# A top-2 mixture-of-experts block behind adapters: GpSimd's row scatters of the first six pairs alternate with its other work

## The chip, the cores and the metric

The kernel runs as one program on one core of a Trainium2 chip. The metric is the device time of one launch in microseconds (us). The kernel before was timed three times; its median is 654.41 us.

## The reference, cut to what matters

There are 16 sequences of 256 tokens with 256 features, 4096 tokens in all. Each sequence picks one of 8 adapters, passes it and a layer norm, and then each token passes a shared feed-forward network and the two best of 8 experts. Only the expressions that the kernel's stages carry out are kept:

```
z = relu(hidden @ Wd + bd)                      # adapter of the sequence, 256 -> 128
y = hidden + z @ Wu + bu
h = (y - mu) * rsqrt(var + eps) * g + b          # layer norm of the adapter's profile
p = softmax(h @ gate_w + gate_b)                 # 8 experts
v, idx = top_k(p, 2);  v = v / (sum(v) + 1e-9)
moe = sum_k v_k * (gelu(h @ ew1[idx_k] + eb1[idx_k]) @ ew2[idx_k] + eb2[idx_k])
out = x + h + gelu(h @ sh_w1 + sh_b1) @ sh_w2 + sh_b2 + moe   # 256 -> 1024 -> 256
```

## The kernel before, in words

All large products are made of fp16 halves: a value is split into a high and a low half, and three products of halves (high-high, high-low, low-high) are summed in fp32.

**Two stages.** The first stage goes through the sequences in eight pairs of 512 tokens (pair p holds sequences 2p and 2p+1). It makes adapter, norm, router and shared network, and writes each token's row (both halves of its normed features, its two expert weights, its number) twice into a table in memory, `xs_rows`, at the place that its two experts give it. The second stage runs the experts over tiles of that table and adds the results into the output.

**Steps.** The first stage is written as a row of steps s = -7 to 31, and each engine runs its own instructions of a step in the written order. Pair p starts at step base(p) = 7p/2 - 7, rounded down, so that about three pairs are in flight. From step 4 on, a step holds for TensorE 12 matmuls of the shared network's first product (L1158), 24 of its second product (L1170), and small work of the pairs. For ScalarE a step holds two GELUs (L554) and the high half of the hidden values (L562). For VectorE it ends with their low half (L966).

**One pair's chain.** The numbers are steps after base(p):

- 0 and 1: GpSimd adds the bias of the adapter to the input (`xb`, L403). TensorE makes down and up products (L1100, L1111).
- 2 and 3: VectorE takes statistics (L734, L737); GpSimd takes the root (`root`, L408).
- 4: VectorE finishes the scales (L752 to L758), ScalarE normalizes (L501).
- 5: VectorE multiplies by the gain (L764), GpSimd adds the norm's bias (`rows`, L413, one instruction for each sequence), ScalarE rounds the high half (L509), which needs both `rows` of the pair.
- 6: VectorE makes the low half (L768), SyncE issues four transposing DMAs (L287), GpSimd adds the residual (`residual`, L417, two instructions) and writes token numbers (L422).
- 8 (7 for the last two pairs): TensorE makes the router's logits (L1124, L1126); they need the transposes and the positions of the pair before (L808). One step later VectorE picks the two experts (L775 to L797) and ScalarE takes the exponentials (L513).
- 11 (10 for the last two): VectorE works out positions and weights (L803 to L832). Then the rows can be scattered.

**The scatters.** `scatter(p, i)` issues two indirect DMAs from GpSimd, one for each of the two experts, for token block i (0 to 3) of pair p (L430). Pair p has eight of them, 64 in all. In the kernel before, the pairs 0 to 5 issue two at the end of each of the steps 11 to 14 after base(p), behind all else that GpSimd has in the step:

```
for i in range(4):
    if s == base(p) + (11 + i if p < NP - 2 else 10 + i // 2):
        scatter(p, i)
```

Where two pairs meet in a step, four stand in a row. The pairs 6 and 7 issue four at the end of each of two steps. Later stages wait for scatters by counting semaphores of the pair's buffer (`d_row`); the buffers of a pair are used again three pairs later.

Of the kernel before, what the change touches and what calls it, by code (L numbers as in the profile page):

```python
# [17 lines left out]
NP = B // 2  # L18
# [20 lines left out]
def at(s, o):  # L39

    return [p for p in range(NP) if s - base(p) == o]
# [34 lines left out]
def adaln_moe(nc, x, xt, ids, wpack, vecs, gnb, gate_w, gate_b, w1, w2, b1, b2, out):  # L76
    ctx = ExitStack()
    with ctx:
# [305 lines left out]
        def gpsimd_program(pool):  # L384
# [21 lines left out]
            def root(p):  # L406
                pool.wait_ge(v_var, p + 1)
                pool.tensor_tensor(rs[:, p % 2, 1, :], rs[:, p % 2, 0, :], half[:, :], ALU.pow).then_inc(q_root, 1)  # L408

            def rows(b):  # L410
                pool.wait_ge(v_t, b + 1)
                y = yb_of(b).rearrange("p (j d) -> p j d", j=2)
                pool.tensor_tensor(y, y, bc(gbs[:, b % 4, 1:2, :], [P, 2, D]), ALU.add).then_inc(q_xn, 1)  # L413

            def residual(b):
                pool.wait_ge(q_xn, b + 1)
                pool.tensor_tensor(acc_of(b), acc_of(b), yb_of(b).rearrange("p (j d) -> p j d", j=2), ALU.add).then_inc(q_acc, 1)  # L417
# [3 lines left out]
                    pool.wait_ge(d_row[p % 3], 16 * 8 * (p // 3))  # L421
                pool.iota(xr[:, p % 3, :, 2 * D + 6:RH].bitcast(I32), pattern=[[P, 4], [0, 1]], base=512 * p, channel_multiplier=1).then_inc(q_tok, 1)  # L422

            def scatter(p, i):
                pool.wait_ge(v_pos, p + 1)
                pool.wait_ge(v_meta, p + 1)
                pool.wait_ge(v_xl, p + 1)
                pool.wait_ge(q_tok, p + 1)
                for q in range(2):
                    pool.indirect_dma_start(xs_d, bass.IndirectOffsetOnAxis(pos[:, p % 3, i, q:q + 1], 0), xr[:, p % 3, i, :].bitcast(I32), None).then_inc(d_row[p % 3], 16)  # L430

            for s in range(FIRST, NS):
                for p in at(s, 3):
                    root(p)
                for p in at(s, 5):
                    rows(2 * p)
                    rows(2 * p + 1)
                for p in at(s, 0):
                    xb(2 * p)
                for p in at(s, 1):  # L440
                    xb(2 * p + 1)
                for p in at(s, 6):
                    residual(2 * p)
                    residual(2 * p + 1)
                    tokens(p)
                for p in range(NP):
                    for i in range(4):
                        if s == base(p) + (11 + i if p < NP - 2 else 10 + i // 2):
                            scatter(p, i)

            def weigh_bias(n):
                pool.wait_ge(v_sel, n + 1)
# [849 lines left out]
```

## Time and profile before

| what | value |
|---|---|
| median of three runs | 654.41 us (653.47 to 654.74) |
| profiled execution | 652.95 us |
| its span, first to last instruction | 650.9 us |
| TensorE busy | 599.8 us, 92% |
| VectorE busy | 503.1 us, 77% |
| GpSimd busy | 413.1 us, 63% |
| ScalarE busy | 389.3 us, 60% |
| granted clock of TensorE, mean of the span | 0.976 |

The profiled execution took 652.95 us, of which 2.05 us lie outside of the span. The first stage lasts until about 243.5 us of the span, the experts take the rest. "Busy" counts an instruction from its recorded start to its recorded end, so time in which a started instruction waits for something inside of the core counts as busy. PE is TensorE, DVE is VectorE, ACT is ScalarE, POOL is GpSimd, and SPq is the DMA queue that SyncE fills.

### The profile page before, as it was taken

How to read it: one execution, taken by the hardware profiler on the slowest of the kernel's cores; microseconds unless marked ns; L12 is line 12 of the kernel's file. 1: busy time of each engine (PE TensorE's matmuls, PEld its weight loads, DVE VectorE, ACT ScalarE, POOL GpSimd, SP SyncE). 2: the span in 40 equal slices, each digit the busy share in tenths (PEclk: the TensorE clock that was granted, in tenths of full speed). 3: DMA queues.
4: the chain of work that ended last, by engine and by line, in shares of the span. 5: the costliest groups of instructions: out<-in, count | busy, mean ns of one | idle time of the engine just before them, and what ended most of it. 6: DMA issues, size and time to landing. Idle time of an engine off the chain costs nothing.

```text
span 650.9 us, 16857 instructions
## 1 busy us (share of the span) xinstructions
PE 599.8 (92%) x5073; PEld 484.5 (74%) x5073; DVE 503.1 (77%) x1198; ACT 389.3 (60%) x662; POOL 413.1 (63%) x320
## 2 busy tenths in 40 slices
PE   4356999999989899999999999999999999999994
PEld 2223666766646668888888888888888888889883
DVE  3859889979975793898989898988896665656883
ACT  1638666667767774667675858576754444434641
POOL 2435687788887601285959585858688575756743
PEclk9768999999989999999999999999999999999998
DMA  7964467666144756367657585666686342424410
GB/s 265 304 145 133 128 190 151 215 195 154 57 126 121 247 160 191 84 125 134 147 105 155 126 142 130 137 133 129 90 71 73 52 73 44 67 41 59 69 26 3
DMA packets 116740, 81.31 MB, mean 125 GB/s; under 512 B 71090, under 2 KB 106162, under 8 KB 116658
## 3 DMA queue, kind: packets, MB, share of 16 engines
q1 hardware_dynamic: 101346, 61.16, 38.4%
q0 software_dynamic: 13296, 16.92, 15.3%
q10 hardware_dynamic: 2016, 2.16, 1.1%
q8 instruction: 48, 0.79, 0.5%
q14 instruction: 34, 0.28, 0.2%
HBM read 43.21 MB, written 24.42 MB: 104 GB/s over the span
## 4 chain that ended last, share of the span: by engine, by line
PE 71%; DVE 9%; issue 7%; POOL 4%; ACT 3%; DMA 3%; SPq 2%; POOLq 0%; ACTq 0%; DVEq 0%
PE H L1219 29%; PE Y L1235 29%; PE Y L1170 6%; PE H L1158 6%; SPq L287 2%; POOL xs_rows L430 2%; DVE wreg L768 1%; DMA xT<-wreg 1%; POOL wreg L413 1%; DVE wreg L737 1%; DMA wreg<-in_wpack 1%; DVE wreg L734 1%; DVE wreg L828 1%; ACT hf L554 1%; ACT wreg L501 1%
## 5 line engine op out<-in xcount | busy, mean ns | idle before, releaser
L608 ACT ACTIVATE hf<-H,prme 128x256 f32<-128x256 f32 (+1 forms) x312 | 151.0, 541 | 112.1 <-issue 97.4
L1219 PE MATMUL H<-xT,wreg 128*128 128x256 f16 (+1 forms) x1872 | 200.4, 263 | 0.2
L1235 PE MATMUL Y<-wreg,hh 128*128 x1136 | 188.6, 273 | 3.6 <-issue 2.4
L1219 PEld LDWEIGHTS H<-xT,wreg 128*128 x1872 | 171.9, 98 | 21.1 <-issue 0.7
L1235 PE MATMUL Y<-wreg,hl 128*128 x568 | 154.8, 273 | 0.0
L1235 PEld LDWEIGHTS Y<-wreg,hh 128*128 128x128 f16 x1136 | 111.0, 98 | 20.6 <-issue 6.1
L1031 DVE SCALAR_TENSOR_TENSOR hl<-hf,prme,hh 128x512 f16<-128x512 f32 (+1 forms) x156 | 115.1, 738 | 5.6
L1029 DVE TENSOR_SCALAR hh<-hf,prme 128x512 f16<-128x512 f32 (+1 forms) x156 | 84.6, 542 | 40.4 <-ACT hf L608 38.3
L457 POOL TENSOR_SCALAR b2w<-b2t,wsel 128x256 f32<-128x256 f32 x71 | 99.1, 1606 | 23.6 <-DMA b2t<-in_b 18.1
L1158 PE MATMUL H<-xT,wreg 128*128 128x512 f16 x384 | 93.8, 396 | 11.8 <-DMA xT<-wreg 11.7
L468 POOL DMA_INDIRECT out_y<-hh,xgm x36 | 64.7, 1799 | 58.0 <-DVE hh L1057 38.9
L468 POOL DMA_INDIRECT out_y<-hl,xgm x35 | 63.6, 1819 | 53.7 <-DVE hl L1057 40.2
L430 POOL DMA_INDIRECT xs_rows<-wreg x64 | 70.1, 1096 | 25.9 <-issue 25.9
L1170 PE MATMUL Y<-wreg,hh 128*128 128x256 f16 x512 | 85.4, 273 | 0.4 <-DVE hl L966 0.4
L1158 PEld LDWEIGHTS H<-xT,wreg 128*128 128x128 f16 x384 | 37.9, 101 | 57.2 <-DMA xT<-wreg 12.8
L1170 PE MATMUL Y<-wreg,hl 128*128 128x256 f16 x256 | 69.8, 273 | 0.0
L554 ACT ACTIVATE hf<-H,prm 128x512 f32<-128x512 f32 x64 | 47.6, 772 | 35.7 <-PE H L1158 28.1
L461 POOL TENSOR_TENSOR b2w<-b2w,xT 128x512 f32<-128x512 f32 (+1 forms) x39 | 53.3, 1367 | 21.9 <-ACT xT L618 19.3
L966 DVE SCALAR_TENSOR_TENSOR hl<-hf,prm,hh 128x1024 f16<-128x1024 f32 x32 | 45.5, 1423 | 25.7 <-ACT hh L562 21.8
L1235 PEld LDWEIGHTS Y<-wreg,hl 128*128 128x128 f16 x568 | 55.6, 98 | 6.0
L1170 PEld LDWEIGHTS Y<-wreg,hh 128*128 128x128 f16 x512 | 50.0, 98 | 12.8 <-issue 1.0
L545 ACT ACTIVATE wreg<-stage,sm 128x2048 f16<-128x2048 f32 x18 | 36.0, 1999 | 38.7 <-DVE prmr L722 23.2
(189 smaller groups left out, 672.9 us busy)
## 6 DMA issues: line engine op xcount, KB each, us to landing
stage<-in_w SPq DMA_DIRECT2D x16, 1024.0 KB
b2t<-in_b SPq DMA_DIRECT2D x39, 128.0 KB
wreg<-in_wpack SPq DMA_DIRECT2D x16, 256.5 KB
wreg<-in_xt SPq DMA_DIRECT2D x16, 256.0 KB
wreg<-in_x SPq DMA_DIRECT2D x16, 256.0 KB, 5.6
wreg<-in_vecs SPq DMA_DIRECT2D x16, 256.0 KB, 4.0
out_y<-wreg SPq DMA_DIRECT2D x16, 256.0 KB, 2.2
xs_rows<-wreg SPq DMA_DIRECT2D x9, 260.0 KB
```

Source lines behind the costliest of these rows:

```text
L430: pool.indirect_dma_start(xs_d, bass.IndirectOffsetOnAxis(pos[:, p % 3, i, q:q + 1], 0), xr[:, p % 3, i, :].bitcast(I32), None).then_inc(d ...
L457: pool.tensor_scalar(b2w[:, n % 2, j, :], b2t[:, n % 3, :], wsel[:, n % 4, 0, j:j + 1], None, ALU.mult).then_inc(q_b2, 1)
L461: pool.tensor_tensor(w, w, b2f[:, 0:blocks(n), :], ALU.add).then_inc(q_b2, 1)
L468: pool.indirect_dma_start(out_rows, bass.IndirectOffsetOnAxis(xgm[:, n % 6, j, 3:4].bitcast(I32), 0), yo_of(n)[:, j, :], None, bounds_chec ...
L554: act.activation(hf[:, g % 4, :], H[g % 3][:, :], ACT.Gelu_apprx_tanh, bias=pr[:, c:c + 1], scale=pr[:, 8:9]).then_inc(a_g, 1)
L608: act.activation(hf[:, c, half * w:(half + 1) * w], H[c][:, half * w:(half + 1) * w], ACT.Gelu_apprx_tanh, bias=pr[:, ch:ch + 1], scale=pr ...
L1029: dve.tensor_scalar(hh[:, n % 2, dst], hf[:, c, 0:w], pr[:, 9:10], None, ALU.mult).then_inc(v_own, 1)
L1031: dve.scalar_tensor_tensor(hl[:, n % 2, dst], hf[:, c, 0:w], pr[:, 9:10], hh[:, n % 2, dst], ALU.mult, ALU.subtract).then_inc(ve_lo, 1)
L1158: m = pe.matmul(H[g % 3][:, :], wsh[:, 0, h, k * 1024 + c * P:k * 1024 + c * P + P], xp[:, a + k, :], start=n == 0, stop=n == 5)
L1170: m = pe.matmul(Y[b % 2][:, j % 2 * D:(j % 2 + 1) * D], hx[:, t % 2, c * 512 + j * P:c * 512 + (j + 1) * P], wsh[:, 1, h, c * D:(c + 1) * ...
L1219: m = pe.matmul(H[c][:, half * w:(half + 1) * w], we[:, bass.ds(e + h * 2048 + k * 1024 + col, P)], xp[:, a + k, 0:w], start=i == 0, stop= ...
L1235: m = pe.matmul(Y[n % 2][:, j * D:(j + 1) * D], hx[:, n % 2, c * w + j * P:c * w + (j + 1) * P], we[:, bass.ds(e + 4096 + h * 2048 + c * D ...
```

## The change

The eight scatters of each of the pairs 0 to 5 are no longer issued two by two at the ends of four steps. They are spread singly over the steps 11 to 15 after base(p), in front of, between and behind the two `rows`, the two `residual`, the `xb` and the `root` that other pairs have in these steps. Even and odd pairs have slots of their own. At most two stand in a row, but for one place with three (steps 20 and 21) and the end of pair 5 (steps 24 and 25), where GpSimd has nothing else left but the scatters of pair 6. An even pair issues its first scatter in step 11 and its last in step 14, an odd pair in the steps 12 and 15. The semaphore waits stand at a pair's first scatter alone. The pairs 6 and 7 issue theirs as before. Nothing is added or removed: 64 scatters and all other instructions are the same.

```diff
-            def scatter(p, i):
-                pool.wait_ge(v_pos, p + 1)
-                pool.wait_ge(v_meta, p + 1)
-                pool.wait_ge(v_xl, p + 1)
-                pool.wait_ge(q_tok, p + 1)
-                for q in range(2):
-                    pool.indirect_dma_start(xs_d, bass.IndirectOffsetOnAxis(pos[:, p % 3, i, q:q + 1], 0), xr[:, p % 3, i, :].bitcast(I32), None).then_inc(d_row[p % 3], 16)
+            def scatter(p, i, q):
+                if (i, q) == (0, 0):
+                    pool.wait_ge(v_pos, p + 1)
+                    pool.wait_ge(v_meta, p + 1)
+                    pool.wait_ge(v_xl, p + 1)
+                    pool.wait_ge(q_tok, p + 1)
+                pool.indirect_dma_start(xs_d, bass.IndirectOffsetOnAxis(pos[:, p % 3, i, q:q + 1], 0), xr[:, p % 3, i, :].bitcast(I32), None).then_inc(d_row[p % 3], 16)
+
+            def even(s, o, i, q):
+                for p in at(s, o):
+                    if p % 2 == 0 and p < NP - 2:
+                        scatter(p, i, q)
 ...
             for s in range(FIRST, NS):
+                even(s, 14, 3, 0)
+                odd(s, 15, 3, 1)
                 for p in at(s, 3):
                     root(p)
+                odd(s, 14, 2, 1)
+                even(s, 13, 1, 1)
                 for p in at(s, 5):
                     rows(2 * p)
+                odd(s, 12, 0, 0)
+                even(s, 12, 0, 1)
+                for p in at(s, 5):
                     rows(2 * p + 1)
+                odd(s, 12, 0, 1)
+                even(s, 12, 1, 0)
                 for p in at(s, 0):
                     xb(2 * p)
                 for p in at(s, 1):
                     xb(2 * p + 1)
+                even(s, 14, 3, 1)
+                odd(s, 12, 1, 0)
+                odd(s, 14, 3, 0)
+                even(s, 11, 0, 0)
                 for p in at(s, 6):
                     residual(2 * p)
+                odd(s, 13, 1, 1)
+                even(s, 13, 2, 0)
+                for p in at(s, 6):
                     residual(2 * p + 1)
                     tokens(p)
-                for p in range(NP):
+                odd(s, 13, 2, 0)
+                even(s, 13, 2, 1)
+                for p in range(NP - 2, NP):
                     for i in range(4):
-                        if s == base(p) + (11 + i if p < NP - 2 else 10 + i // 2):
-                            scatter(p, i)
+                        if s == base(p) + 10 + i // 2:
+                            scatter(p, i, 0)
+                            scatter(p, i, 1)
```

`odd` is written like `even`, for the odd pairs. Only GpSimd's order changes; the other engines keep theirs.

On GpSimd, the steps 7 to 9 before read as follows (L430 is a scatter, L403 `xb`, L413 `rows`, L417 `residual`; the four scatters are the last two of pair 0 and the first two of pair 1):

```order
L403 TENSOR_TENSOR wreg<-wreg 128x512
L430 DMA xs_rows<-wreg 35072x260 x4
L413 TENSOR_TENSOR wreg<-wreg 128x512 x2
L403 TENSOR_TENSOR wreg<-wreg 128x512
L430 DMA xs_rows<-wreg 35072x260 x2
L417 TENSOR_TENSOR wreg<-wreg 128x512 x2
L422 IOTA wreg 128x4
```

The same place on GpSimd now (the first row holds pair 0's sixth and seventh scatter):

```order
L430 DMA xs_rows<-wreg 35072x260 x2
L403 TENSOR_TENSOR wreg<-wreg 128x512
L430 DMA xs_rows<-wreg 35072x260
L413 TENSOR_TENSOR wreg<-wreg 128x512
L430 DMA xs_rows<-wreg 35072x260
L413 TENSOR_TENSOR wreg<-wreg 128x512
L430 DMA xs_rows<-wreg 35072x260
L403 TENSOR_TENSOR wreg<-wreg 128x512
L430 DMA xs_rows<-wreg 35072x260
L417 TENSOR_TENSOR wreg<-wreg 128x512
L430 DMA xs_rows<-wreg 35072x260
L417 TENSOR_TENSOR wreg<-wreg 128x512
```

The run of three two-input instructions (two L413 and an L403) and the run of two L417 are gone; each of them now has a scatter directly in front of it. Steps 14 to 16 read alike in both kernels, with pairs 2 and 3 in the place of 0 and 1.

On GpSimd, the steps 11 to 13 before (pair 2's first six scatters around pair 4's `rows` and `residual`):

```order
L403 TENSOR_TENSOR wreg<-wreg 128x512
L430 DMA xs_rows<-wreg 35072x260 x2
L413 TENSOR_TENSOR wreg<-wreg 128x512 x2
L430 DMA xs_rows<-wreg 35072x260 x2
L408 TENSOR_TENSOR wreg<-wreg 128x4
L417 TENSOR_TENSOR wreg<-wreg 128x512 x2
L422 IOTA wreg 128x4
```

The same place now:

```order
L403 TENSOR_TENSOR wreg<-wreg 128x512
L430 DMA xs_rows<-wreg 35072x260
L413 TENSOR_TENSOR wreg<-wreg 128x512
L430 DMA xs_rows<-wreg 35072x260
L413 TENSOR_TENSOR wreg<-wreg 128x512
L430 DMA xs_rows<-wreg 35072x260
L408 TENSOR_TENSOR wreg<-wreg 128x4
L430 DMA xs_rows<-wreg 35072x260
L417 TENSOR_TENSOR wreg<-wreg 128x512
L430 DMA xs_rows<-wreg 35072x260
L417 TENSOR_TENSOR wreg<-wreg 128x512
L422 IOTA wreg 128x4
```

One scatter has moved between the two `rows` of the pair, and one between its two `residual`.

## Rows read from the trace of the kernel before

**Rows 1.** Windows: span, then PE, PEld, DVE, ACT, POOL busy us, PEclk, DMA

```profile
90.00:178.00 88.00, 85.95 (x623) 59.42 (x624) 79.19 (x196) 60.22 (x79) 70.74 (x60) 1.00 0.62 168
...
186.00:197.00 11.00, 11.00 (x66) 6.66 (x65) 4.90 (x21) 7.66 (x9) 9.86 (x10) 0.84 0.32 104
```

**Rows 2.** Timeline of PE, instructions behind idle time [us <-releaser]

```profile
90.84 1.47 PE L1158 MATMUL H<-xT,wreg 128*128 128x512 f16 x6 [0.88 <-DMA xT<-wreg]
...
162.22 0.19 PE L1124 MATMUL H<-wreg,xT 128*128 128x16 f16 x2 [0.85 <-DVE wreg L808]
...
173.62 0.39 PE L1170 MATMUL Y<-wreg,hh 128*128 128x256 f16 x2 [0.36 <-DVE hl L966]
...
185.14 0.21 PE L1124 MATMUL H<-wreg,xT 128*128 128x16 f16 x2 [3.17 <-DMA xT<-wreg]
```

**Rows 3.** Chain that ended last, two steps behind the longest wait

```profile
185.69 4.30 PE H L1158 x12
...
192.61 2.59 PE H L1158 x12
```

**Rows 4.** Timeline of POOL and DVE, the long waits for the port

```profile
94.91 0.96 POOL L430 DMA_INDIRECT xs_rows<-wreg  x1 [0.30 <-issue]
95.64 5.06 DVE L966 SCALAR_TENSOR_TENSOR hl<-hf,prm,hh 128x1024 f16<-128x1024 f32 x1 [1.27 <-issue]
95.88 2.50 POOL L413 TENSOR_TENSOR wreg<-wreg 128x512 f32<-128x512 f32 x2
98.32 1.28 POOL L403 TENSOR_TENSOR wreg<-wreg 128x512 f32<-128x512 f32 x1
...
102.28 4.15 DVE L768 SCALAR_TENSOR_TENSOR wreg<-wreg,sm 128x1024 f16<-128x1024 f32 x1
...
150.88 3.16 DVE L789 TENSOR_TENSOR wreg<-wreg 128x64 f32<-128x64 uint32 x1
```

**Rows 5.** Timeline of POOL and DVE, L828 twice

```profile
137.08 0.96 POOL L430 DMA_INDIRECT xs_rows<-wreg  x1 [0.30 <-issue]
137.56 1.81 DVE L828 TENSOR_TENSOR wreg<-wreg 128x4 f32<-128x4 f32 x1
138.06 1.27 POOL L403 TENSOR_TENSOR wreg<-wreg 128x512 f32<-128x512 f32 x1
...
182.31 0.96 POOL L430 DMA_INDIRECT xs_rows<-wreg  x1 [0.30 <-issue]
182.81 0.17 DVE L828 TENSOR_TENSOR wreg<-wreg 128x4 f32<-128x4 f32 x1
183.58 1.70 POOL L430 DMA_INDIRECT xs_rows<-wreg  x1 [0.30 <-issue]
```

**Rows 6.** Groups of POOL, 68 to 197 us: busy us, mean ns of one

```profile
L417 POOL TENSOR_TENSOR wreg<-wreg 128x512 f32<-128x512 f32 x12 | 19.4, 1633 | 0.1
L413 POOL TENSOR_TENSOR wreg<-wreg 128x512 f32<-128x512 f32 x12 | 15.7, 1332 | 2.3 <-DVE wreg L764 2.0 <-issue 0.2
L403 POOL TENSOR_TENSOR wreg<-wreg 128x512 f32<-128x512 f32 x9 | 12.0, 1336 | 0.1
```

**Rows 7.** Timeline around pair 2's `rows`, POOL and DVE

```profile
74.55 1.26 POOL L413 TENSOR_TENSOR wreg<-wreg 128x512 f32<-128x512 f32 x1 [0.52 <-DVE wreg L764]
74.75 1.61 DVE L764 TENSOR_TENSOR wreg<-wreg 128x512 f32<-128x512 f32 x1 [0.29 <-ACT wreg L501]
76.44 1.27 POOL L413 TENSOR_TENSOR wreg<-wreg 128x512 f32<-128x512 f32 x1 [0.63 <-DVE wreg L764]
```

**Rows 8.** Timeline around pair 4's `rows`, POOL, ACT and PE

```profile
123.16 2.86 POOL L413 TENSOR_TENSOR wreg<-wreg 128x512 f32<-128x512 f32 x2 [0.86 <-DVE wreg L764]
126.05 1.15 ACT L509 ACTIVATE wreg<-wreg,sm 128x1024 f16<-128x1024 f32 x1 [2.62 <-POOL wreg L413]
129.92 2.75 PE L1158 MATMUL H<-xT,wreg 128*128 128x512 f16 x12
130.06 1.44 ACT L554 ACTIVATE hf<-H,prm 128x512 f32<-128x512 f32 x2
```

More of the change, by code:

```diff
@@ L422, in tokens, with odd @@
                 pool.iota(xr[:, p % 3, :, 2 * D + 6:RH].bitcast(I32), pattern=[[P, 4], [0, 1]], base=512 * p, channel_multiplier=1).then_inc(q_tok, 1)
-            def scatter(p, i):
-                pool.wait_ge(v_pos, p + 1)
-                pool.wait_ge(v_meta, p + 1)
-                pool.wait_ge(v_xl, p + 1)
-                pool.wait_ge(q_tok, p + 1)
-                for q in range(2):
-                    pool.indirect_dma_start(xs_d, bass.IndirectOffsetOnAxis(pos[:, p % 3, i, q:q + 1], 0), xr[:, p % 3, i, :].bitcast(I32), None).then_inc(d_row[p % 3], 16)
+            def scatter(p, i, q):
[9 more added lines that the diff above has]
+                        scatter(p, i, q)
+            def odd(s, o, i, q):
+                for p in at(s, o):
+                    if p % 2 and p < NP - 2:
+                        scatter(p, i, q)
             for s in range(FIRST, NS):
+                even(s, 14, 3, 0)
+                odd(s, 15, 3, 1)
                 for p in at(s, 3):
                     root(p)
+                odd(s, 14, 2, 1)
+                even(s, 13, 1, 1)
                 for p in at(s, 5):
                     rows(2 * p)
+                odd(s, 12, 0, 0)
+                even(s, 12, 0, 1)
+                for p in at(s, 5):
                     rows(2 * p + 1)
+                odd(s, 12, 0, 1)
+                even(s, 12, 1, 0)
                 for p in at(s, 0):
```

## Prediction

> **What bounds the kernel now.** I read the windows first. From 90 to 178 us TensorE is busy 85.95 of 88 us at full clock, with VectorE at 79.19 and GpSimd at 70.74 close behind [rows 1]. So TensorE sets the pace, and what another engine loses counts only where TensorE comes to wait for it. The timeline of TensorE, read for rows with idle time, gives these places: 0.88 us at 90.84 for the transposes of pair 2, 0.85 at 162.22 for positions (L808), 0.36 at 173.62 for VectorE's low half, and 3.17 at 185.14 for the transposes of pair 6 [rows 2]. Behind the last one the 12 matmuls of a step take 4.30 us instead of 2.59 [rows 3], and the granted clock of that stretch is 0.84 [rows 1]: part of it ran at the lower of the two levels. That is 1.71 us more for the same wait. All in all these waits cost 0.88 + 0.85 + 0.36 + 3.17 + 1.71 = 6.97 us. They are the most that a better order could win here, and the end of the kernel follows TensorE's steps: behind 197 us the first stage, and then the experts, are paced by TensorE, so I carry a shift at 197 us to the end unchanged.
>
> **How GpSimd and VectorE meet.** The timelines of the two, laid side by side, show the thing that the change acts on. VectorE's L966 takes about 1.28 us; the one at 95.64 took 5.06. It began 0.73 us into a scatter (94.91), and GpSimd had two L413 and one L403 behind that scatter, which ended at 99.60. L966 ended 1.10 us later: it did its work only then [rows 4]. L768 at 102.28 (4.15 us) and L789 at 150.88 (3.16 us for work of 0.2) went the same way, each behind a scatter and two L417. L828 shows it for a single instruction: at 137.56, 0.48 us into a scatter with an L403 behind it, it takes 1.81 us and ends with the L403; at 182.81, 0.50 us into a scatter with another scatter behind it, it takes 0.17 [rows 5]. So a scatter by itself lets VectorE's two-input instructions pass, but a two-input instruction of GpSimd that stands directly behind a scatter closes the way already about 0.5 us before its own recorded start. The other way round, the scatter at 183.58 takes 1.70 us instead of 0.96, since L966 started at 183.17 was running [rows 5].
>
> The Trainium skill ("SBUF — State Buffer", section "Who interferes with whom") says of the port pair that the two engines share that whoever issues first holds it for the whole instruction. It gives no early closing: by that page an L828 that starts ahead of the L403 would pass, and the trace says 1.81 us. The same section infers that a two-input tensor_tensor does not hold up descriptor generation; the 1.70 us above speak against that for this form. By the page alone the change would only shorten runs, which is the first rival below.
>
> **The change part by part.**
>
> *Shorter runs: a gain.* The runs of two and three, behind which VectorE waited longest, now have a scatter between each two. In the three long cases VectorE lost (5.06 - 1.28) + (4.15 - 1.28) + (3.16 - 0.2) = 9.6 us [rows 4]. With one instruction per run a wait is at most 0.55 + 1.25 = 1.8 us, so 5.4 for three. Gain: 4.2 us of VectorE's time.
>
> *More early closings: a loss.* Between 68 and 197 us GpSimd has 12 + 12 + 9 = 33 of these instructions [rows 6], 1.25 us each without waits (2.50 for the two at 95.88, [rows 4]), 41 us. Read against the order, 10 of the 33 stood directly behind a scatter and did not wait for anything. Now 31 of 33 do; I take 27, since four `rows` will find their gain not yet made. That is 17 more early closings of 0.55 us, 9.4 us. The way was closed for 41.3 + 5.5 = 46.8 us, now for 56.2, a fifth more. I added up what VectorE's instructions took above their own shortest in this stretch: about 23 us in 17 waits, of which the rows shown carry 11.2. If waits grow with the closed time, that is +4.7 us. Against the 4.2 from above, VectorE loses 0.5 us. VectorE is what TensorE waits for at 162.22 and 173.62, and it stands in the chain of the transposes too; it has no slack to hide this, so I take all of it: **+0.5**.
>
> *Scatters that wait.* A VectorE instruction that waited for GpSimd's port starts when that one ends, and the next thing on GpSimd is now a scatter, which then waits for VectorE: 0.74 us longer in [rows 5] (1.70 against 0.96), and at most 1.28. A fifth more than 17 waits is three to four more, and of the old ones those inside a run had no scatter behind them. Some five longer scatters are 3.7 to 6.4 us on GpSimd, which stands in the chain through `rows` (L413). GpSimd is busy 70.74 of 88 us, so a part is absorbed; at 0 it would cost nothing, at full price 6. I take a small part: **+1.0**.
>
> *Pair 2's `rows`.* The second L413 began at 76.44 since it waited for the gain (L764), which itself waited for the first L413 [rows 7]. The scatter now between the two starts when the first ends, at 75.81; with gaps of 0.2 and 0.96 us the second L413 begins at about 76.97, 0.5 us later. ScalarE's L509, VectorE's L768 and the transposes follow in line, and TensorE already waits for them, 0.88 us at 90.84: **+0.5**. It is nothing if VectorE is late there for other reasons.
>
> *Pair 4's `rows`.* The two L413 at 123.16 end at 126.02 and release L509 at 126.05 [rows 8]. With a scatter between them they end 0.96 + 0.2 = 1.15 us later, and so do L509, the exponentials and the two GELUs behind it, which ran from 130.06. The first GELU ends at 130.78 and frees the bank that the second half of TensorE's step needs; TensorE, at 129.92 + 1.30 = 131.22, came 0.44 us after that. Now it waits 1.15 - 0.44 = 0.7 us: **+0.7**. If the gain of pair 4 comes earlier, because VectorE was not held at 95 and 102 us, this is nothing.
>
> *At no cost:* a pair's last scatter. Its buffer is used again by L509 three pairs on, which stands in step base + 15 for an even pair and base + 16 for an odd one. The last scatter now stands in step base + 14 and at the start of base + 15, so a whole step remains for it to land, and a step is more than two of the 2.59 us groups [rows 3]. If it were too short, L509 would wait by some tenths. The scatters of pair 6 and 7 begin when their weights are there, not when GpSimd is free, so what is ahead of them does not move them.
>
> **The sum.** 0.5 + 1.0 + 0.5 + 0.7 = +2.7 us on the profiled execution's 652.95 us, so 655.65 us. The median of the runs is 1.46 us above the profiled one, so I expect 657.1 us, 0.4% slower.
>
> **Rivals.**
>
> *Faster.* The early closing matters little between a scatter and a single instruction, because the way opens again each 2.4 us, and the three long waits simply go: 4.2 us of VectorE's time. Then the waits of 0.85 and 0.36 us vanish, the 3.17 us shrink by 1.3 or more, and TensorE may not fall to the lower clock (1.71 us): 0.85 + 0.36 + 1.3 + 1.71 = 4.2 us, 650.2 us. For it speaks that the long waits are plainly there and are over a third of all. Against it speaks that TensorE had no idle time between 91 and 162 us in spite of two of them. It wins where VectorE's total wait falls by over 2 us.
>
> *Much slower.* GpSimd may keep the way closed from one instruction through the scatter to the next, as it does over a run of three [rows 4]. No row shows a single scatter between two ready two-input instructions. Then each of some 20 scatters closes 0.6 us more, 12 us. Half or two thirds of it on the path, on top of 2.7, is +9: 663.4 us.
>
> *No change.* The gains and losses of VectorE cancel, and GpSimd's waits are absorbed: only one of the two `rows` terms stays, at most 0.7 us, or a gain of that size meets it. 654.4 us. It is also what happens if instructions of VectorE meet GpSimd's at other points than I think, in both directions.
>
> **How the numbers follow.** A difference under 0.2%, 1.3 us, can't be told from no change. My forecast gets 0.43, its own range being 655.9 to 660. Faster gets 0.27, no change 0.19, much slower 0.11. So slower in all is 0.54. The range from 650.6 to 661.0 leaves out most of the much slower case and the best part of the faster one, some 0.2.
>
> **What would show it.** Right: in the new timeline L828 and L966 take 1.8 to 2.5 us in more places than before and never 3 or more; scatters of 1.5 us and above become common; TensorE waits over 1.2 us at 91 us, has a new wait of the kind L1158 <- ScalarE at about 130 us, and its wait for L808 near 163 us is above 0.85; the wait for pair 6's transposes stays near 3 us with the slow group behind it. Wrong: VectorE's excess falls well below 23 us, or the wait at 185 us shrinks below 2 us and the slow group is gone (faster); or VectorE has waits of 3 us across a scatter (much slower).

## The result and the profile after

The changed kernel takes 658.62 us (median of 4 runs, 658.08 to 659.19), the kernel before 654.4 us (4 runs, 653.47 to 654.74): a ratio of 1.0067, 95% interval 1.0049 to 1.0084. It is 4.2 us slower; the profiled execution took 658.54 us, with a span of 656.6 us and a mean granted clock of 0.972. Measured again later, beside other runs of the kernel before (kernel 9 below), it took 658.01 us (12 runs), a ratio of 1.0053 (1.0031 to 1.0075).

In the changed file the lines of the engines other than GpSimd stand 29 further down: L966 is now L995, L808 L837, L1124 L1153, L1158 L1187. GpSimd's L403 to L430 keep their numbers.

TensorE's timeline after, rows with idle time, as [rows 2] shows them for before:

```profile
92.41 2.76 PE L1187 MATMUL H<-xT,wreg 128*128 128x512 f16 x12 [1.16 <-DMA xT<-wreg]
96.19 0.39 PE L1199 MATMUL Y<-wreg,hh 128*128 128x256 f16 x2 [1.02 <-DVE hl L995]
...
134.51 0.82 PE L1187 MATMUL H<-xT,wreg 128*128 128x512 f16 x3 [0.38 <-ACT hf L583]
...
149.95 0.39 PE L1199 MATMUL Y<-wreg,hh 128*128 128x256 f16 x2 [0.47 <-DVE hl L995]
...
168.44 0.20 PE L1153 MATMUL H<-wreg,xT 128*128 128x16 f16 x2 [3.11 <-DVE wreg L837]
...
191.95 0.21 PE L1153 MATMUL H<-wreg,xT 128*128 128x16 f16 x2 [2.60 <-DMA xT<-wreg]
```

The waits sum to 8.74 us, against 0.88 + 0.85 + 0.36 + 3.17 = 5.26 us before. The big change is in one place: the wait for the positions (L808 before, L837 now) grew from 0.85 to 3.11 us. Behind it the granted clock fell as well, to 0.83 over ten microseconds, where before it was 1.00 until 178 us [rows 1]. The windows of after, columns as in [rows 1], the first and last answering to its two rows, the middle one around the grown wait:

```profile
92.00:180.00 88.00, 82.61 (x582) 56.40 (x583) 80.39 (x193) 54.29 (x72) 71.56 (x58) 0.98 0.58 164
...
166.00:176.00 10.00, 7.56 (x46) 4.83 (x47) 9.65 (x22) 3.94 (x8) 7.84 (x7) 0.83 0.24 81
...
192.00:203.00 11.00, 11.00 (x75) 6.61 (x76) 9.29 (x25) 7.25 (x9) 9.35 (x9) 0.84 0.35 121
```

In the chain that ended last, the group of 12 behind the transposes takes 3.99 us now and a normal one 2.59, against 4.30 and 2.59 in [rows 3]:

```profile
192.50 3.99 PE H L1187 x12
...
199.42 2.59 PE H L1187 x12
```

To compare many kernels I use one stretch of TensorE's timeline, from the start of pair 1's ranking (the first matmul of L1136 before, L1165 after) to that of pair 6. Before, and then after:

```profile
83.47 0.18 PE L1136 MATMUL H<-wreg 1*128 1x32 f16 x1
...
197.75 0.18 PE L1136 MATMUL H<-wreg 1*128 1x32 f16 x1
```

```profile
84.76 0.18 PE L1165 MATMUL H<-wreg 1*128 1x32 f16 x1
...
204.56 0.18 PE L1165 MATMUL H<-wreg 1*128 1x32 f16 x1
```

That is 114.28 and 119.80 us, 5.5 us more. The spans differ by 5.7 us. The other parts nearly cancel: the changed kernel comes 1.3 us late to the start of the stretch, after two groups of the start-up that took longer, ahead of any scatter, and it makes up 1.1 us behind its end. So the two profiles lie 1.5 us further apart than the medians, which differ by 4.2 us. The stretch by itself swings by 1 to 2 us between executions of one kernel (119.80 and 118.46 for the changed one, 114.42 and 116.40 for the one with the rows together), so it shows where 4 us go, not 1 us.

VectorE and GpSimd meet more often now. The timeline of both, and ScalarE's L538, around pair 5's two `rows` (L413):

```profile
147.18 1.64 POOL L413 TENSOR_TENSOR wreg<-wreg 128x512 f32<-128x512 f32 x1 [1.09 <-DVE wreg L793]
147.61 2.29 DVE L995 SCALAR_TENSOR_TENSOR hl<-hf,prm,hh 128x1024 f16<-128x1024 f32 x1
148.97 1.79 POOL L430 DMA_INDIRECT xs_rows<-wreg  x1 [0.16 <-issue]
...
150.80 1.28 POOL L413 TENSOR_TENSOR wreg<-wreg 128x512 f32<-128x512 f32 x1
...
152.11 1.15 ACT L538 ACTIVATE wreg<-wreg,sm 128x1024 f16<-128x1024 f32 x1 [4.70 <-POOL wreg L413]
152.24 0.99 POOL L430 DMA_INDIRECT xs_rows<-wreg  x1 [0.17 <-issue]
...
153.25 1.29 POOL L403 TENSOR_TENSOR wreg<-wreg 128x512 f32<-128x512 f32 x1
153.29 2.34 DVE L797 SCALAR_TENSOR_TENSOR wreg<-wreg,sm 128x1024 f16<-128x1024 f32 x1 [1.09 <-ACT wreg L538]
```

The scatter at 148.97 finds VectorE's L995 running and takes 1.79 us. The second L413 therefore starts 3.62 us behind the first. L538, which waits for both, starts at 152.11. VectorE's L797 behind it takes 2.34 us, and this is no early closing: the L403 had started 0.04 us ahead of it. Further on, the same VectorE queue, late by then, does a low half (L995), pair 6's roots and pair 4's positions:

```profile
157.97 0.99 POOL L430 DMA_INDIRECT xs_rows<-wreg  x1 [0.16 <-issue]
...
158.52 2.84 DVE L995 SCALAR_TENSOR_TENSOR hl<-hf,prm,hh 128x1024 f16<-128x1024 f32 x1
...
158.99 1.28 POOL L417 TENSOR_TENSOR wreg<-wreg 128x512 f32<-128x512 f32 x1
...
163.33 2.01 POOL L408 TENSOR_TENSOR wreg<-wreg 128x4 f32<-128x4 f32 x1 [1.09 <-DVE wreg L776]
...
165.53 1.04 POOL L430 DMA_INDIRECT xs_rows<-wreg  x1 [0.20 <-issue]
...
165.76 0.16 DVE L785 SCALAR_TENSOR_TENSOR wreg<-wreg 128x4 f32<-128x4 f32 x1
165.96 1.95 DVE L787 SCALAR_TENSOR_TENSOR wreg<-wreg 128x4 f32<-128x4 f32 x1
166.60 1.27 POOL L403 TENSOR_TENSOR wreg<-wreg 128x512 f32<-128x512 f32 x1
167.83 0.21 DVE L832 TENSOR_TENSOR wreg<-wreg,H 128x64 f32<-128x64 f32 x1
168.05 0.99 POOL L430 DMA_INDIRECT xs_rows<-wreg  x1 [0.17 <-issue]
168.07 0.22 DVE L837 TENSOR_REDUCE wreg<-wreg 128x8 int32<-128x64 f32 x1
```

Two early closings of the kind of [rows 5] stand here on the way to L837, for which TensorE waits until 168.44. The L995 started 0.47 us ahead of the second L417 and takes 1.57 us more than the shortest one. L785 and L787 are alike, and L787 takes 1.79 us more: it started 0.64 us ahead of the L403 and ended with it.

I added up, as for the prediction, what VectorE's instructions took above the shortest of their kind between 60 and 205 us. It was 23.3 us in 17 waits, the longest of 3.79. It is 35.6 us in 27 waits, none over 1.79. Seven of the 17 (16.2 us) began while a scatter ran with a two-input instruction behind it, so they are early closings, and 15 of the 27 (24.6 us). The others began while a two-input instruction of GpSimd was already running: 10 (7.1 us) before, 12 (11.0 us) after.

The trace of after also shows how early the closing comes. I took VectorE's instructions with both inputs in SBUF (their rows name no PSUM tile such as H, U or Y) that began while a scatter ran with a two-input instruction ready behind it. There are 38. The 14 that were held began 0.17 to 0.66 us ahead of that instruction, the 24 that passed 0.68 to 1.04 us ahead. Of the 13 that began during a scatter with another scatter behind it, none was held.

### The profile page after: what moved, and what is told of

Read it like the earlier page. It is cut to its first block, busy times and chain, and to the rows that moved or that the text cites. A ratio compares the mean times of both kernels' runs of the same rounds, so it can differ in the third digit from the quotient of the medians.

```text
span 656.6 us, 16809 instructions
## 1 busy us (share of the span) xinstructions
PE 603.5 (92%) x5073; PEld 486.9 (74%) x5073; DVE 512.6 (78%) x1198; ACT 389.8 (59%) x662; POOL 415.3 (63%) x320
## 4 chain that ended last, share of the span: by engine, by line
PE 70%; DVE 9%; issue 6%; POOL 6%; ACT 3%; DMA 3%; SPq 2%; POOLq 0%; DVEq 0%; ACTq 0%
PE H L1248 28%; PE Y L1264 28%; PE Y L1199 5%; PE H L1187 5%; POOL xs_rows L430 3%; SPq L287 2%; POOL wreg L417 1%; DMA xT<-wreg 1%; ACT wreg L530 1%; DVE wreg L797 1%; PE Z L1129 1%; PE U L1140 1%; DVE wreg L766 1%; DMA wreg<-in_wpack 1%; DVE wreg L763 1%
## 5 line engine op out<-in xcount | busy, mean ns | idle before, releaser
L1187 PE MATMUL H<-xT,wreg 128*128 128x512 f16 x384 | 94.3, 398 | 12.4 <-DMA xT<-wreg 12.0
L430 POOL DMA_INDIRECT xs_rows<-wreg x64 | 75.9, 1186 | 20.2 <-issue 19.9
L1187 PEld LDWEIGHTS H<-xT,wreg 128*128 128x128 f16 x384 | 38.0, 101 | 58.0 <-DMA xT<-wreg 13.1
L995 DVE SCALAR_TENSOR_TENSOR hl<-hf,prm,hh 128x1024 f16<-128x1024 f32 x32 | 52.8, 1651 | 23.2 <-ACT hh L591 23.0
```

What stands on the lines that cost most here:

```text
L995: dve.scalar_tensor_tensor(hl[:, t % 2, q * 1024:(q + 1) * 1024], hf[:, g % 4:g % 4 + 2, :].rearrange("p a n -> p (a n)"), pr[:, 9:10], hh ...
L1187: m = pe.matmul(H[g % 3][:, :], wsh[:, 0, h, k * 1024 + c * P:k * 1024 + c * P + P], xp[:, a + k, :], start=n == 0, stop=n == 5)
```

## The experiments

Two theories. **A**: the loss is VectorE's time to early closings, in which GpSimd shuts it out while a scatter in front of a two-input instruction still runs. **B**: the loss is the scatter between a pair's two `rows`, which makes the second one late. The runs below are in the order in which they were made: kernels 1 to 4, 5 to 8, 9 to 11 and 12, each group on a chip of its own, with runs of the kernel before on the same chip. "Stretch" is the 114.28 us from above; "excess" is VectorE's sum.

**1 to 3. A wait behind the scatters.** GpSimd writes a mark behind each run of scatters and waits for it, so that the next instruction can't be taken up before the scatter is done. Kernel 1 has it in the changed kernel, kernel 3 in the kernel before; kernel 2 is kernel 1 without the waits. The marks are additional work of 0.12 us each.

```diff
+            def mark():
+                if state["scattered"]:
+                    k = state["marks"]
+                    pool.memset(marks[:, k:k + 1], 0.0).then_inc(q_mark, 1)
+                    state["marks"] = k + 1
+                    pool.wait_ge(q_mark, k + 1)
+                state["scattered"] = False
...
             def xb(b):
+                mark()
...
             def scatter(p, i, q):
+                state["scattered"] = True
```

(`root`, `rows` and `residual` begin with `mark()` too; kernel 2 lacks the line with `wait_ge`.)

> The changed kernel, in which GpSimd, before each two-input instruction or root that stands behind a scatter, first writes a small mark behind that scatter and waits until it is written. The scatter is then over before the next instruction can start. Theory A (a two-input instruction behind a scatter closes the shared port about 0.5 us ahead of its own start): VectorE instructions that begin during a scatter pass, L828 and L966 no longer wait across the end of a scatter, VectorE's excess falls from about 35 us in the changed kernel to under 28, the time falls from 658.6 to about 656.5 to 657.5, since each mark costs some 0.2 us of GpSimd. Theory B (the early closing is harmless, the loss is that a scatter between the two rows instructions makes a pair late): the marks only add some 27 x 0.2 us to GpSimd, so 658.6 to 660.

> The same small marks at the same places, without the wait: the control of the kernel with waits. Theory A: the next instruction is still taken up while the scatter runs, the early closing stays, so the time is at least that of the changed kernel, 658.6 to 660. Theory B: the same. If this one is as fast as the kernel with waits, the wait is not what matters but the write between the two.

> The kernel before with marks and waits behind its scatters, at some ten places that count. Theory A: the four L828 waits of 1.6 us go, but L966, L768 and L789, which began during a scatter, now pass too; VectorE's excess falls from 23 us to under 16. TensorE's waits of 0.85 us and part of those of 3.17 and 1.71 us go: 651.5 to 654. Theory B: nothing to win there, 654.4 to 656, as GpSimd gets some 20 small waits more.

Measured: kernel 1 661.96 us, ratio 1.0113 (1.0088 to 1.0138); kernel 2 661.5 us, 1.0101 (1.0073 to 1.0129); kernel 3 658.04 us, 1.0019 (0.9986 to 1.0051). All three times lie above what either theory gave. The excess fell to 11.3 us in kernel 1 and 11.2 us in kernel 3, and stayed at 36.0 us in kernel 2. So the wait does take the early closings away, and the mark alone does not: in kernel 1 all 39 of VectorE's two-input instructions that began during a scatter with a mark behind it passed. The stretch was 110.5, 118.6 and 114.1 us. Kernel 3 speaks against A for the old order: the excess is halved, yet TensorE's wait for the positions is 0.86 us (0.85 before), that for pair 6's transposes 3.16 (3.17 before), and the stretch is as long as before. Kernel 1's stretch is 9.3 us shorter than the changed kernel's, and yet its time was no better. The reason stands behind that point in its trace. TensorE's timeline of kernel 1:

```profile
209.62 0.38 PE L1204 MATMUL H<-xT,wreg 128*128 128x512 f16 x1 [0.23 <-issue]
210.33 0.39 PE L1204 MATMUL H<-xT,wreg 128*128 128x512 f16 x1 [0.33 <-issue]
211.04 0.38 PE L1204 MATMUL H<-xT,wreg 128*128 128x512 f16 x1 [0.32 <-issue]
...
217.43 1.01 PE L1204 MATMUL H<-xT,wreg 128*128 128x512 f16 x2 [1.52 <-issue]
```

From 209 to 218 us TensorE issued at first only one matmul each 0.71 us, though it waited for no other engine; a group that takes 2.59 us took 9.2. The granted clock was still 1.00 from 209 to 212 us and 0.50, the lower of its two levels, from 215 to 221, so the pause came first, and the slower clock added to it. Seven of the profiles of kernels 1 to 8 have idle time of this kind somewhere between 209 and 224 us, 0.8 us in kernel 2, 1.5 in kernel 8 and several us in the other five: from pair 6's ranking to pair 7's these five take 23.0 to 29.1 us, where the kernels before and changed take 16.6 and 16.4. The kernel before was spread from 653.3 to 662.4 us on these two chips. The profiles of kernels 9 to 12, of the kernel before and of the changed one have no such pause. So the times of kernels 1 to 8 are blurred by several us, and I lean on their stretches, which end ahead of the pause.

**4. The two `rows` together.** The changed kernel, with the scatter from between a pair's two `rows` moved behind the second.

```diff
                     rows(2 * p)
+                    rows(2 * p + 1)
                 odd(s, 12, 0, 0)
                 even(s, 12, 0, 1)
-                for p in at(s, 5):
-                    rows(2 * p + 1)
```

> The changed kernel, but the two rows instructions of a pair stand together again and the scatter that stood between them comes right behind. Theory A: about six early closings of some 27 fewer and six runs of two again: a small part of the loss goes, 657 to 658.3. Theory B (a pair's rows are late by one scatter): the whole loss of 4.2 us goes, 653.5 to 655.5, TensorE's new wait at about 134 us for ScalarE's GELU disappears and so does most of the wait at 168 us for L808.

Measured: 662.66 us, ratio 1.0082 (1.0041 to 1.0123), with the pause in its profile; of the eight runs two are at 655.3 and 656.5 and six above 661.8. The stretch is 114.4 us, the excess 31.7 us in 25 waits. TensorE's wait for the positions is 1.16 us instead of 3.11. The time is in neither theory's range. The kernel keeps most early closings, and its stretch is the old one again: for B, with the time still open.

**5. Wait and `rows` together.** Both edits, 1 and 4, in one kernel.

> The changed kernel with both of the earlier edits: a mark and a wait behind a run of scatters before GpSimd's next two-input operation, and each pair's two rows operations next to each other again. Measured from the first ranking of a pair by TensorE to the sixth, the kernel before takes 114.3 us in its profile, the changed one 119.8, the changed one with the wait 110.5 and the one with the rows together 114.5. Theory A (what the change loses is VectorE time to early closings of the port, and the wait takes it away whatever the order is): that stretch takes 109 to 111 us here, and where TensorE's issue isn't disturbed around 210 us, as it was for 6 us in three of the four profiles of the last call, the run takes 653 to 656 us. Theory B (what it loses is the lateness of pairs' second rows): the stretch takes about 110 us as well, but then the wait adds nothing to what rows together give, and the stretch would be 113 to 115 us. So below 112 speaks for A, above 113 for B.

Measured: 658.33 us, ratio 1.002 (0.999 to 1.0049); stretch 111.5 us, excess 18.0 us. Below 112, which spoke for A: on the stretch the wait gives 3 us beyond what the rows together give. The time, with the pause in its profile, is above the 653 to 656 us that A gave without one.

**6. The split alone.** The kernel before with one scatter of the pair in step 12 between the two `rows`, all others in their old places.

```diff
                     rows(2 * p)
+                for p in at(s, 12):
+                    if p < NP - 2:
+                        scatter(p, 1, (0,))
+                for p in at(s, 5):
                     rows(2 * p + 1)
...
-                            scatter(p, i)
+                            scatter(p, i, (1,) if p < NP - 2 and i == 1 else (0, 1))
```

> The kernel before with one part of the change alone: a single scatter of the pair that is being scattered stands between a pair's two rows operations; all others stay where they were. Theory B (the split of the rows carries the loss, since with it each second row comes 1 to 1.8 us later): 656.5 to 658.5 us and a new wait of TensorE near 91 us above 0.9 us. Theory A (the loss is the early closings, which follow the number of scatters that have a GpSimd two-input operation right behind them, here 5 more against 20 more in the changed kernel): 654.4 to 655.5 us, and about 3 us more of VectorE's excess than before's 23 us.

Measured: 656.54 us, ratio 0.9989 (0.9956 to 1.0021); stretch 114.7 us, excess 25.4 us. TensorE's wait near 91 us did grow, to 1.61 us, and there is no wait at all for the positions. The time in us lies at the lower edge of what B gave, but the kernel before took 657.27 us on this chip. So B in its plain form falls: the split by itself costs nothing that can be measured.

**7 and 8. Half of the pairs each.** The changed kernel, with only the even or only the odd pairs in the new slots and the others in the old ones.

```diff
             def odd(s, o, i, q):
+                return
...
-                for p in range(NP - 2, NP):
+                for p in range(NP):
                     for i in range(4):
-                        if s == base(p) + 10 + i // 2:
+                        if (p >= NP - 2 or p % 2 == 1) and s == base(p) + (11 + i if p < NP - 2 else 10 + i // 2):
```

(For kernel 8, `even` and `p % 2 == 0`.)

> The changed kernel with only pairs 0, 2 and 4 in the new slots; pairs 1, 3 and 5 are scattered as before. Both theories have the large wait of the changed kernel at 168 us come from pair 4's neighbourhood (roots of pair 5's rows, with an early closing of 1.79 us at 165.96 while an even pair's scatters run), so this half should keep most of the loss: 657 to 658.5 us, TensorE's wait near 165 us at 2 us or more. If the loss is spread evenly over the pairs it is 656 to 656.5 us.

> The changed kernel with only pairs 1, 3 and 5 in the new slots; pairs 0, 2 and 4 are scattered as before. By the same reading this half should lose little: 654 to 655.5 us, and TensorE's wait near 163 us stays below 1.2 us. Evenly spread: 656 to 656.5 us.

Measured: even pairs 664.35 us, ratio 1.0101 (1.0063 to 1.0138), stretch 117.2 us; odd pairs 658.49 us, 0.9998 (0.9965 to 1.0031), stretch 114.3 us. That the odd pairs carry nothing came as expected, by ratio and stretch. The even ones carry 2.9 of 5.5 us in the stretch, so the rest comes only when both halves are changed; TensorE's wait for the positions is 1.30 us, where 2 or more was expected. Their time is worse than the changed kernel's own ratio. Their profile has a pause at 216 to 219 us and 2.76 us of wait for pair 6's transposes; even their fastest run is at 660.2 us. Why, stays open.

**9 to 11. The changed kernel again, the rows together again, and the wait at some places only.** In kernel 11 the mark and the wait stand ahead of `rows` and `xb` alone, not of `root` and `residual`.

```diff
             def root(p):
-                mark()
...
             def residual(b):
-                mark()
```

> The changed kernel itself, unaltered, on the chip of this call, so that the times of the other two can be set beside it: on the last two chips the kernel before was spread from 653 to 662 us, where its first four runs lay within 1.3 us. If the pauses of TensorE's issue near 210 us that seven of the eight profiles of those chips show are the chips' own, this kernel has them too and its runs spread upward from about 658; the stretch from the first to the sixth ranking of a pair stays at 119 to 120.5 us. If they belong to the altered kernels, its runs lie within 2 us of 658.6 again.

> The changed kernel with each pair's two rows operations together, once more, since six of its eight runs were in the paused group. Theory B (the split of the rows, on top of the early closings, carries the loss): the fastest runs at 655 to 656.5 us, 2 to 3 us under the fastest of the unaltered changed kernel beside it, and the stretch at 114 to 115 us. Theory A (the early closings alone carry it, and these remain): fastest runs within 1 us of the changed kernel's, at 657.5 to 658.5.

> The changed kernel with a mark and a wait behind the scatters only where one of the two rows operations or the addition of the residual input (xb) comes next, not ahead of the roots and of the residual sums. The early closings named as costly are those from the split rows into VectorE's low rows (153.29 us, 1.07 us) and from a scatter through xb into the roots (165.96 us, 1.79 us), so theory C (a conjunction: the split costs only where VectorE is closed out as well) expects the wait of TensorE at 168 us to fall from 3.1 to below 1 us and the stretch to 111.5 to 114.5 us, with fastest runs at 654.5 to 656. If all early closings count alike, a third of them remain and the stretch is 114 to 117 us.

None of the three profiles has the pause between 205 and 225 us. Since this is another chip, that does not decide whether the pause belongs to the chips or to the altered kernels. On this chip, with 12 runs each and 29 of the kernel before:

| kernel | median us | ratio to before | 95% interval | stretch us | excess us |
|---|---|---|---|---|---|
| before | 654.28 | | | | |
| 9, changed | 658.01 | 1.0053 | 1.0031 to 1.0075 | 118.5 | 35.9 |
| 10, rows together | 654.14 | 0.9991 | 0.9972 to 1.0010 | 116.4 | 31.4 |
| 11, some waits | 651.88 | 0.9954 | 0.9932 to 0.9975 | 110.4 | 19.1 |

Moving one scatter per pair from between the two `rows` takes the whole loss away by the time; its fastest run (652.15 us) is 3 us under the changed kernel's (655.10), as B said, though its profile, from one of its slower runs, has a stretch only 2.1 us shorter. And with the split left in place, the wait at `rows` and `xb` takes the loss away too, and 2.4 us more: kernel 11 beats both kernels, with a stretch and a fastest run (649.86 us) below what theory C gave. Its timeline at the places shown for after (L427 is `rows`, L445 the scatter, L416 `xb`, L553 and L812 the high and low rows, L852 the positions):

```profile
145.06 1.86 POOL L427 TENSOR_TENSOR wreg<-wreg 128x512 f32<-128x512 f32 x1
...
147.07 0.99 POOL L445 DMA_INDIRECT xs_rows<-wreg  x1 [0.15 <-issue]
...
148.06 0.12 POOL L403 MEMSET marks<- 128x1 f32 x1
148.27 1.26 POOL L427 TENSOR_TENSOR wreg<-wreg 128x512 f32<-128x512 f32 x1
149.56 1.15 ACT L553 ACTIVATE wreg<-wreg,sm 128x1024 f16<-128x1024 f32 x1 [3.57 <-POOL wreg L427]
...
150.68 0.12 POOL L403 MEMSET marks<- 128x1 f32 x1
150.74 1.29 DVE L812 SCALAR_TENSOR_TENSOR wreg<-wreg,sm 128x1024 f16<-128x1024 f32 x1 [2.64 <-ACT wreg L553]
...
161.42 1.04 POOL L445 DMA_INDIRECT xs_rows<-wreg  x1 [0.20 <-issue]
...
161.85 0.16 DVE L802 SCALAR_TENSOR_TENSOR wreg<-wreg 128x4 f32<-128x4 f32 x1
...
162.18 0.22 DVE L852 TENSOR_REDUCE wreg<-wreg 128x8 int32<-128x64 f32 x1
...
162.47 0.12 POOL L403 MEMSET marks<- 128x1 f32 x1
162.67 1.26 POOL L416 TENSOR_TENSOR wreg<-wreg 128x512 f32<-128x512 f32 x1
```

The low rows take 1.29 us instead of 2.34, the last root instruction (L802) 0.16 instead of 1.95, and TensorE's matmuls behind L852 have no idle time in front of them. The second `rows` still starts 3.21 us behind the first. Set against the start of pair 4's ranking in each profile, VectorE's queue stands like this (us; the low half is L966 before, L995 in the changed kernel, the positions are L808 and L837):

| kernel | low rows start | next low half starts, takes | positions start | TensorE waits for them |
|---|---|---|---|---|
| before | -6.8 | -0.2, 1.28 | 7.1 | 0.85 |
| changed | -5.5 | -0.2, 2.84 | 9.3 | 3.11 |
| 10, rows together | -7.7 | -3.6, 2.83 | 7.4 | 1.15 |
| 11, some waits | -6.0 | -0.7, 1.28 | 5.5 | none |

In kernel 10 the two closings of the changed kernel are there unchanged, on the low half and on the last root, but the queue comes to them 3.3 us earlier. In kernel 11 the split is there and the closings are not. The one on the low half went although no wait stands at `residual`: there VectorE came 0.82 us ahead of GpSimd's instruction instead of 0.47. In the kernel before, the queue is as late at the low half as in the changed one, since L789 had been held for 2.95 us [rows 4]; but there the low half passes, as the scatter during which it begins has another scatter behind it. This is a conjunction of A and B: the split makes VectorE's queue late, and the closings keep it late until TensorE asks for the positions. Which of the two kinds of places, `rows` or `xb`, gives the 2.4 us, and whether the same waits gain as much with the rows together, was not measured.

**12. The same waits in the kernel before.** Edit 11 in the old order.

> The kernel before with the same selective mark and wait that took the changed kernel to 651.9 us, 2.4 us under the kernel before on that chip: behind scatters, only where a rows operation or xb comes next. If the gain is the wait's alone (any order of scatters profits), this kernel is as fast, a ratio of 0.993 to 0.998 and a stretch from the first to the sixth ranking of 110 to 112 us. If it takes the change's alternation as well, whose short runs leave no long hold on the port, the ratio is 0.998 to 1.002 and the stretch stays at 113.5 to 114.5 us, as it did with the wait everywhere (114.1 us); my expectation is this second case.

Measured: 653.92 us, before 653.45 us, ratio 1.0001 (0.9979 to 1.0024); stretch 114.7 us, excess 18.1 us. The wait gives nothing in the old order, the case that I expected, although the excess falls as far; the stretch is 0.2 us above its range. So the gain of kernel 11 needs both the change's spreading and the wait.

## Why the prediction was right, and where its steps were not

The forecast of 657.1 us, slower by 0.4%, was 1.5 us under the measured 658.62. Its direction came from a mechanism that the runs confirm; the terms were not well sized, and the closeness of the number is in part luck. The sum gave +2.7 us on the profiled execution, and the profiled executions differ by 5.6 (652.95 and 658.54). Half of that miss was hidden by the 1.46 us that I added from the profiled execution to the median: for the changed kernel they differ by 0.08.

TensorE's account of the stretch is simple. What is left of it without its waits and without the time lost to the lower clock (the length times one minus the granted clock) is 107.3 us within 0.6 us in all fourteen profiles. Some of them:

| kernel | stretch | waits | of these for VectorE | lower clock | rest |
|---|---|---|---|---|---|
| before | 114.3 | 5.3 | 1.2 | 1.7 | 107.3 |
| changed | 119.8 | 8.7 | 4.6 | 3.4 | 107.7 |
| 9, changed again | 118.5 | 7.8 | 4.6 | 3.4 | 107.3 |
| 10, rows together | 116.4 | 6.0 | 2.6 | 3.4 | 107.0 |
| 11, some waits | 110.4 | 3.2 | none | none | 107.2 |
| 3, before with waits | 114.1 | 5.2 | 0.9 | 1.7 | 107.3 |

So of the 5.5 us, 3.5 are waits, nearly all for VectorE, and 1.7 are a second drop of the clock.

*Shorter runs, more early closings (+0.5).* Both halves are in the trace: no VectorE wait is over 1.79 us, where 1.8 was the bound, and the closings are more. But the two did not cancel. The count of early closings was good: ready two-input instructions right behind a scatter went from 10 to 26, and I had said 27. The step from there to time was not. I let the waits grow with the closed time, by a fifth; the waits at early closings went from 7 to 15 and the excess grew by 12.3 us instead of 0.5. And I took all of VectorE's loss as TensorE's, since VectorE had no slack. Kernel 3 shows that in the old order it had: the excess fell by 12 us, and TensorE's waits stayed. What TensorE waited for VectorE went from 0.85 + 0.36 = 1.21 us [rows 2] to 1.02 + 0.47 + 3.11 = 4.60 us. So together with the next term I had 1.5 us where 3.4 came.

*Scatters that wait (+1.0).* Right in kind and in size on GpSimd; how much of it reached TensorE no run separates. The groups of POOL from 70 us on, before and then after (columns as in [rows 6]):

```profile
L430 POOL DMA_INDIRECT xs_rows<-wreg x47 | 52.0, 1107 | 16.7 <-issue 16.7
```

```profile
L430 POOL DMA_INDIRECT xs_rows<-wreg x44 | 54.7, 1243 | 12.1 <-issue 11.8 <-POOL wreg L417 0.3
```

A scatter takes 136 ns more on average, 6 us over 44, the upper end of the 3.7 to 6.4 us that I gave. Those of 1.5 us and more went from 6 to 11, the five more that I had taken.

*Pair 2's `rows` (+0.5).* The wait went from 0.88 to 1.16 us, so +0.3; with the rows together it was 0.26 and 0.59 us in two profiles. Shown.

*Pair 4's `rows` (+0.7).* The new wait for ScalarE came at 134.51 us with 0.38 us, and is in neither profile with the rows together. Shown, at half the size.

*The missing term.* The sum had no entry for pair 5's `rows`, the place of the largest loss: 3.11 - 0.85 = 2.3 us of wait, and with the 1.7 us of lower clock behind it 4.0 us, more than the whole sum. I had looked only at pairs whose successors TensorE waited for before, and took the position wait at 162 us as fed by average VectorE losses. The runs show that it is fed by that split, through L538 and L797, together with two closings, one on a low half (L995) and one on the roots.

*The wait for pair 6's transposes* was to stay near 3 us. It is 2.60 us, 0.6 us less, probably because TensorE itself came later. The group of 12 behind it takes 3.99 us instead of 4.30, but the matmuls behind that group are slower in return: the lower clock costs 1.7 us there in both profiles.

*The faster rival* said that the long waits simply go, and that 4.2 us with them. They did go, but in this order their place was taken by more short ones. Its world exists nonetheless: kernel 11, with 5 early closings instead of 15, is at 0.9954. *The much slower rival* (the port shut across a scatter) is refuted: no wait of after is above 1.79 us. *No change* is what kernel 10 shows, with one scatter per pair placed otherwise.

The Trainium skill ("SBUF — State Buffer", section "Who interferes with whom") says that issue order decides who blocks. The scatter at 148.97 us, 1.79 us long beside the L995 that started first, agrees with that, and speaks again, as [rows 5] did, against carrying the section's inference that a two-input tensor_tensor leaves descriptor generation alone over to this form (a scalar_tensor_tensor). Kernels 1 and 2 fit the rule if a GpSimd instruction counts as issued while the scatter ahead of it still runs: the mark changes nothing without its wait. On why it could be, the Trainium skill ("Perfetto Trace Analysis", section "DMA Instruction — SWDGE (GPSIMD)") says that descriptors are written by two of GpSimd's processors and that the instruction goes into a queue of each; the others would then be free to take up the next one. No run here shows GpSimd's single processors, so this is a reading, not a finding.

## What to carry to other kernels

On GpSimd, a ready two-input instruction directly behind a scatter held VectorE's instructions with both inputs in SBUF that began up to 0.66 us ahead of it in the changed kernel; count such neighbours before spreading scatters between other work. The sum of what VectorE loses doesn't give the time, though: follow its queue to the instruction that TensorE waits for. Don't put a scatter between two operations whose common successor another engine's queue waits for, unless the queue has slack: here it made that queue 3.3 us late, counting the wait that it ran into. Where spreading is wanted anyway, a tiny write with a wait on it behind the scatter keeps the port open. At two kinds of places it made the changed kernel 0.9% faster; at all places it shortened the stretch as much (110.5 us), but its time there was taken on a chip with the pause and shows no gain; in the old order it gave nothing that could be measured.

## What the runs showed of the hardware that was not expected

- The early closing needs no more than the next instruction being ready, and a small write between it and the scatter doesn't prevent it: excess 36.0 us with a mark but no wait, 11.3 us with the wait. A mark with its wait costs GpSimd about 0.2 us: in kernel 11 the scatter ends at 148.06 us and the next `rows` starts at 148.27.
- On the chips of kernels 1 to 8 TensorE paused between matmuls, in kernel 1 with one or two matmuls each 0.71 us or a multiple of it, for up to 8 us, between 209 and 224 us of the span, with no engine or DMA named as releaser and no instruction transfer landing in that time in kernel 1. It seems bound to the time, not to a place in the program: in kernel 1 it ends 5 us ahead of pair 7's ranking, in kernel 8 it falls on that ranking, at 217.5 us. The granted clock fell to 0.50 during the pause of kernel 1 and came back behind it. Its cause wasn't found.
- Ahead of the first scatter, where all the kernels are alike, the profiles differ by up to 2.9 us: the matmuls that follow at 62.45 us in the kernel before start at 64.39 and 65.31 us in two profiles of the changed one. A start-up group of 12 takes 4.35 us before and 5.30 after; the granted clock is 0.50 from 30 to 40 us in all of them.
